# A mixture-of-experts decoder layer on one core: the experts' first matmul as three fp32r products, with their split weights streamed through a ring

## The chip, the cores and the metric

The kernel runs on one core of one Trainium2 chip. The metric is the device time of that core in microseconds, from one launch; lower is better. Engines are called by the names of the profile: PE is TensorE (PEld its weight loads), DVE is VectorE, ACT is ScalarE, POOL is GpSimd, SP is SyncE, whose queue issues most of the DMAs.

## The reference, cut to what matters

One decoder layer for 4 sequences of 512 tokens of width 256: causal attention, block-sparse cross attention of 16 heads, and a mixture of 8 experts with top-2 routing beside a shared expert. All in float32. The last part is the one that changes:

```python
xf = x.reshape(-1, DIM)                      # 2048 tokens x 256
logits = xf @ gate_w + gate_b
top_w, top_i = jax.lax.top_k(logits, K)      # 2 of 8 experts for each token
gw = jax.nn.softmax(top_w, axis=-1)
combine = (gw[:, :, None] * jax.nn.one_hot(top_i, E)).sum(axis=1)
for e in range(E):                           # w1[e]: 256 x 1024, w2[e]: 1024 x 256
    h = jax.nn.gelu(xf @ w1[e] + b1[e], approximate=False)
    out = out + combine[:, e:e + 1] * (h @ w2[e] + b2[e])
shared = jax.nn.gelu(xf @ ws1 + bs1, approximate=False) @ ws2 + bs2
return (out + shared).reshape(orig_shape)    # a layernorm follows
```

## The kernel before, in words

Every engine has a program of its own, written out by hand, and the engines meet at semaphores. There is no scheduler: an engine's instructions run in the order in which the code issues them.

**Attention.** Four "bodies" (`body(b, first, last)`), one for each sequence. Each does the cross attention of sequence b in two halves and between them the first attention of sequence b+1; at its end stands `project2`, which makes the queries, keys and values of the next body. In `project2` PE waits for `cb_out` before it spreads the queries (the matmul of L1570): `cb_out` is the end of `combine` on DVE (L1150 to L1161), which joins the outputs of the heads in `attn`. POOL splits the inputs of the next sequence into a high fp32r part and the rest (`split`, L422 and L425), adds a bias to the values (L508), helps in the layernorms (L479, L491, L494), and ends a body with `keep_x1` (L484) and `keep_x2` (L499).

**Three products.** In attention and in the shared expert a float32 product is made of three fp32r products: both operands are split into hi and lo, and `mm3` (L250) adds hi x hi, hi x lo and lo x hi in PSUM. The routed experts don't do so before: their matmuls (L1809, L1829) take float32 operands as they are.

**Shared expert.** The tokens go through it in 8 chunks of 256 (`shared_hidden`, `shared_output`). ACT does the gelu, DVE the splits (`x_split`, `h_split`, with `lo_of`, L861) and the sums (`y_out`). Its PE work covers the routing: DVE computes from the gate logits each token's slots (L1263 to L1313), then POOL scatters the 2048 rows twice to their slots in DRAM, 128 rows for each of 32 indirect DMAs (L582, the tile `slot_rows`), with at most four under way. SP then loads the first two tiles of rows (`xs`, L391), PE turns them (`turn_x`, L1792), and `shared_output` of the last chunk follows.

**Routed experts.** 4096 rows, sorted by expert and padded to tiles of 128, make TILES = 39 tiles; all 39 are computed. For a tile t PE does, in this order, `hidden(t+1)` (4 float32 matmuls of 512 columns, L1809; each is two records in the trace), `turn_x(t+2)` (2 transposes, L1792), `output(t)` (8 float32 matmuls of 256 columns, L1829) and `turn_h(t+1)` (8 transposes of `hp`, L1820). ACT copies the turned rows to `xT`, applies the gelu to the turned hidden rows (L815) and weights the result (L824); DVE copies the hidden rows out of PSUM (L1330) and adds the bias of the second layer (L1338); POOL adds the weighted rows to `row_sum` in DRAM (L597). The expert of a tile stands in `table`; PE loads it to a register (`expert(t)`) and addresses `we`, which holds all weights of all 8 experts (2 MB each), by it. SP loads experts 0 and 1 at the end of attention, experts 2 to 7 when the last chunk of the shared expert is done.

Of the kernel before, what the change touches and what calls it, by code (L numbers as in the profile page):

```python
# [54 lines left out]
EARLY = 2  # L55

# [16 lines left out]
def build(nc, x_d, xT_d, cT_d, w_d, brow_d, bcol_d, gate_w_d, gate_b_d,  # L73
          w1_d, b1T_d, w2_d, b2_d, ws1_d, bs1T_d, ws2_d, bs2_d, out_d):
    ctx = ExitStack()
    with ctx:  # L76
# [3 lines left out]
        def sem(name):  # L80
# [6 lines left out]
        q_rows = nc.dram_tensor("q_rows", (2, P, S), F, kind="Internal").ap()  # L87
        row_sum = nc.dram_tensor("row_sum", (T + P, D), F, kind="Internal").ap()
# [30 lines left out]
        shared = ExitStack()  # L119
        prod = sb("prod", [P, NT, D], F, shared)  # L120
        shared.close()
        v_s = sb("v_s", [P, 2, NT, D], FR, att)
        pT_s = sb("pT_s", [P, 2, NT * (NT + 1) // 2, P], FR, att)
# [6 lines left out]
        shift0 = sb("shift0", [P, 2], F, att)  # L130
        at_s = q_s
# [38 lines left out]
        we = sb("we", [P, E, EW], F, mo)  # L170
# [4 lines left out]
        xT = sb("xT", [P, 2, KD, P], F, mo)  # L175
# [22 lines left out]
        table = sb("table", [P, TILES], I32, mo)  # L198
        mo.close()
# [4 lines left out]
        sb("w2_home", [P, 24 * D], F, sh)  # L204
        ws1_s = sb("ws1_s", [P, 2, KD * HID], FR, sh)
        sb("at_home", [P, 2 * KD * S], F, sh)
        ws2_s = sb("ws2_s", [P, 2, NH * D], FR, sh)
        h_s = sb("h_s", [P, 2, NH, CT], FR, sh)
        h_full = sb("h_full", [P, NH, CT], F, sh)
# [12 lines left out]
        names = """x0_in x_in qk_in w1_in w2_in w1_hi w1_lo m_ps shift_step wvo_ps bvo bq_set bias_in b_in x_raw_in c_raw_in wsplit wsplit_hi consts consts2 masks q_zero xbo pad_set pad_out  # L222
          xa_split qk1_ps qk1_hi qk1_lo v1_ps v1_hi v1_lo s1_ps s1_raw s1_max s1_exp p1_den
          pt_ps pt_hi pt_lo w1_ps ln_res ln_step ln_pow x1_out x2_sub x2_out x_kept k_ones
          x1_ps x1_hi x1_lo ctx_split qk2_ps qk2_hi qk2_lo aug_in v_set
          a_ps a_red aug_step aug_ready augT_ps augT_out b_ps b_exp pv_done oc_out os_out
          sel_set parity_set sel_ps sel_act sel_dve
          cb_ps w_exp cb_step cb_out v2_ps v2_out at_ps at_hi at_lo w2_ps
          g_ps g_out lg_ps lg_out lgT_ps lgT_out
          ws_in we_in eb_in r_step r_exp r_exp_in r_ps table_ready slots_ready  # L230
          ws_split sxT_ps sx_split sh_ps sh_out sh_split sh_used sy_ps sy_sum sy_out kept_out
          xT_ps xT_out meta_in gate_set h_ps h_out hT_ps hT_out y_ps y_sum y_out y_idx
          f_step f_var f_pow f_bias f_out o_sent
# [4 lines left out]
        st_sent = [sem(f"s_st_sent{q}") for q in range(4)]  # L238
        k_away = [sem(f"s_k_away{h}_{part}") for h in range(2) for part in ("hi", "lo")]
# [16 lines left out]
        def _(sp):  # L256
# [21 lines left out]
            sp.wait_ge(s["pad_set"], 4)  # L278
# [42 lines left out]
            def body(b, first, last):  # L321
# [18 lines left out]
                if first:  # L340
                    sp.wait_ge(s["q_zero"], 1)
                else:
                    sp.wait_ge(s["b_ps"], 2 * UNITS * (2 * b))
# [21 lines left out]
            def load_expert(e):  # L365
# [6 lines left out]
            for e in range(EARLY):  # L372
                load_expert(e)
# [43 lines left out]
        def _(pool):  # L417
# [83 lines left out]
            def body(b, first, last):  # L501
# [20 lines left out]
                if not first:  # L522
                    keep_x2(b - 1)
# [1393 lines left out]
```

## Time and profile before

| | |
|---|---|
| median of 3 runs | 805.07 us (804.23 to 806.89) |
| the profiled execution | 804.36 us, span from first to last instruction 802.6 us |
| PE busy | 742.9 us, 93% of the span |
| DVE busy | 405.8 us, 51% |
| ACT busy | 331.6 us, 41% |
| POOL busy | 218.7 us, 27% |
| mean granted clock of TensorE | 0.969 |
| HBM read and written | 45.57 and 25.11 MB |

Read from it: PE is the engine that the whole program hangs on, from about 40 us to 780 us; the other engines matter where PE waits for them. Times in rows are microseconds from the first instruction.

### The profile page before, as it was taken

The page shows a single profiled execution, that of the slowest core. Times are in us where ns is not written, and L with a number is a line of the kernel's source. Part 1 is how long each engine was busy: PE and PEld are TensorE (multiplying, and loading weights), DVE is VectorE, ACT ScalarE, POOL GpSimd, SP SyncE. Part 2 cuts the span into 40 slices and gives each one's busy share as a digit, 9 for nine tenths or more (in the row PEclk, how much of TensorE's full clock was granted, in tenths as well). Part 3 has the DMA queues.
Part 4 walks back from the last instruction along what each step waited for, and adds up shares of the span by engine and source line. Part 5 has one row for each costly group of instructions (what it writes and reads, how often), then busy time and mean ns, then how long its engine had stood idle before and what let it go on. Part 6 is the DMA issues. An engine that isn't in the chain of part 4 may idle for free. (4 is left out here: it accounts for less than half of the span.)

```text
span 802.6 us, 14818 instructions
## 1 busy us (share of the span) xinstructions
PE 742.9 (93%) x4804; PEld 563.6 (70%) x4805; DVE 405.8 (51%) x807; ACT 331.6 (41%) x885; POOL 218.7 (27%) x217
## 2 busy tenths in 40 slices
PE   6689999999999999999999899999999999999960
PEld 5567666967696766669999856767676767676740
DVE  3767788787879766667875321212121212121214
ACT  1232556456636654463332124343434343434324
POOL 5762212151214103002078201212121212121223
PEclk9987999999999999999999999999999999999985
DMA  9952331405050713032133499412121212121216
GB/s 289 250 152 54 56 110 40 84 27 148 0 108 0 226 29 55 7 134 88 63 114 112 95 318 311 96 27 40 26 39 26 39 26 39 26 39 26 27 15 215
DMA packets 60489, 71.76 MB, mean 89 GB/s; under 512 B 15264, under 2 KB 49952, under 8 KB 59552
## 3 DMA queue, kind: packets, MB, share of 16 engines
q1 hardware_dynamic: 47968, 57.03, 25.8%
q0 software_dynamic: 7152, 9.34, 7.1%
q10 hardware_dynamic: 5328, 4.85, 2.2%
q8 instruction: 25, 0.41, 0.2%
q14 instruction: 16, 0.13, 0.1%
HBM read 45.57 MB, written 25.11 MB: 88 GB/s over the span
## 5 line engine op out<-in xcount | busy, mean ns | idle before, releaser
L815 ACT ACTIVATE hT<-ps,b1T 128x128 f32<-128x128 f32 x312 | 84.8, 383 | 167.2 <-PE ps L1820 167.1
L1829 PE MATMUL ps<-we,hT 128*128 x624 | 142.9, 383 | 2.5 <-ACT hT L815 2.5
L1809 PE MATMUL ps<-we,xT 128*128 x312 | 140.5, 593 | 0.3 <-issue 0.3
L1829 PEld LDWEIGHTS ps<-we,hT 128*128 128x128 f32 x624 | 117.0, 192 | 17.6 <-issue 3.2
L1330 DVE COPY hp<-ps 128x512 f32<-128x512 f32 x78 | 50.3, 686 | 146.5 <-PE ps L1809 146.5
L1103 DVE TENSOR_REDUCE mx<-ps 128x4 f32<-128x512 f32 (+1 forms) x128 | 103.6, 819 | 20.6 <-PE ps L1627 19.4
L1809 PEld LDWEIGHTS ps<-we,xT 128*128 128x128 f32 x312 | 56.3, 191 | 56.4 <-issue 56.4
L726 ACT ACTIVATE pT<-ps 128x256 f32<-128x256 f32 x128 | 49.1, 384 | 69.7 <-PE ps L1643 59.5
L1627 PE MATMUL ps<-k_stack,q_stack 96*128 96x256 f32 (+1 forms) x256 | 72.3, 368 | 5.2 <-DVE mx L1103 3.0
L592 POOL CAST yidx<-meta 128x1 int32<-128x1 f32 x39 | 7.2, 184 | 234.8 <-ACT yw L824 234.8
L597 POOL DMA_INDIRECT row_sum<-yw,yidx x39 | 60.9, 1560 | 30.5 <-issue 26.4
L1338 DVE TENSOR_TENSOR ysum<-ps,b2b 128x256 f32<-128x256 f32 x39 | 16.6, 425 | 103.3 <-PE ps L1829 103.3
L1627 PEld LDWEIGHTS ps<-k_stack,q_stack 96*128 96x128 f32 x256 | 40.1, 197 | 33.4 <-issue 19.1
L729 ACT ACTIVATE pT<-ps 128x256 f32<-128x256 f32 (+1 forms) x128 | 62.4, 487 | 0.1
L250 PE MATMUL ps<-ws_s,h_s 128*128 128x256 f32 x384 | 48.6, 288 | 0.0
L250 PE MATMUL ps<-xT_s,ws_s 128*128 128x256 f32 x384 | 48.2, 285 | 0.0
L250 PEld LDWEIGHTS ps<-ws_s,h_s 128*128 128x128 f32 x384 | 47.7, 196 | 0.0
L250 PEld LDWEIGHTS ps<-xT_s,ws_s 128*128 128x128 f32 x384 | 46.6, 192 | 0.2 <-issue 0.2
L1649 PE MATMUL ps<-q_stack,k_stack 98*128 98x256 f32 (+1 forms) x128 | 46.3, 362 | 0.0
L582 POOL DMA_INDIRECT slot_rows<-XW,slot_tab x32 | 36.8, 1150 | 30.1 <-DVE slot_tab L1313 20.9
L775 ACT ACTIVATE h_full<-ps,b1T 128x256 f32<-128x256 f32 x64 | 26.4, 473 | 39.5 <-PE ps L250 39.5
L1820 PE MATMUL ps<-ident,hp 128*128 128x128 f32 x312 | 40.5, 273 | 1.4 <-DVE hp L1330 1.4
(238 smaller groups left out, 1083.7 us busy)
## 6 DMA issues: line engine op xcount, KB each, us to landing
we<-in_w SPq DMA_DIRECT2D x16, 1024.0 KB, 8.9
k_stack<-k_rows SPq DMA_DIRECT2D x24, 256.0 KB, 4.8
slot_rows<-attn SPq DMA_DIRECT2D x1, 4992.0 KB, 24.5
xs<-slot_rows ACTq DMA_DIRECT2D x37, 128.0 KB, 2.0
k_rows<-k_s SPq DMA_DIRECT2D x16, 256.0 KB, 2.1
q_stack<-q_rows SPq DMA_DIRECT2D x48, 64.0 KB, 5.6
x_raw<-in_xT SPq DMA_DIRECT2D x4, 512.0 KB, 5.1
XW<-in_x SPq DMA_DIRECT2D x4, 512.0 KB, 8.5
```

The source lines that it names most:

```text
L250: m = nc.tensor.matmul(out, lhs(a), rhs(b), start=first and n == 0, stop=last and n == 2, skip_group_check=check)
L597: pool.indirect_dma_start(out=row_sum, out_offset=bass.IndirectOffsetOnAxis(ap=yidx[:, q, :], axis=0), in_=yw[:, q, :], in_offset=None, co ...
L726: nc.scalar.activation(pT[:, m % 2, u % 2, 0:2 * P], ps[:, bank, 256:512], ACT.Exp, scale=SCALE2)\
L729: nc.scalar.activation(pT[:, m % 2, u % 2, 2 * P:2 * P + w], ps[:, bank + 1, 0:w], ACT.Exp, scale=SCALE2).then_inc(s["b_exp"], 1)
L815: last = nc.scalar.activation(hT[:, c, :], ps[:, 4 + c // 4, (c % 4) * P:(c % 4 + 1) * P], ACT.Gelu, bias=b1T[:, bass.ds(e * NH + c, 1)])
L1103: nc.vector.tensor_reduce(mx[:, i, 2 * p:2 * p + 2, r0:r0 + nb], ps[:, 2 * ((u + flip) % 2):2 * ((u + flip) % 2) + 2, 0:nb * P].rearrange( ...
L1330: last = nc.vector.tensor_copy(hp[:, c * 512:(c + 1) * 512], ps[:, 2 + c, :])
L1627: m = nc.tensor.matmul(ps[:, 2 * ((u + flip) % 2) + j, 0:nb * P], q_stack[0:96, ha * HALF + PAIRS * j + p, n * P:(n + 1) * P], k_stack[0:9 ...
L1649: nc.tensor.matmul(ps[:, bank + 1, 0:w].rearrange("p (h n q) -> p h n q", h=2, q=P), k_stack[0:98, p, i * P:(i + 1) * P], qv[0:98, :, :].r ...
L1809: m = nc.tensor.matmul(ps[:, 2 + c, :], xT[:, q, k, :], w[:, bass.ds(e, 1), k * HID + c * 512:k * HID + (c + 1) * 512].rearrange("p o n -> ...
L1820: m = nc.tensor.transpose(ps[:, 4 + c // 4, (c % 4) * P:(c % 4 + 1) * P], hp[:, c * P:(c + 1) * P], ident[:, :])
L1829: m = nc.tensor.matmul(ps[:, 6, 0:D], hT[:, c, :], w[:, bass.ds(e, 1), KD * HID + c * D:KD * HID + (c + 1) * D].rearrange("p o n -> p (o n)"),
```

## The change

The first layer of the routed experts (`hidden`) becomes three fp32r products with `mm3`, like the shared expert's. For that the weights w1 of each expert must lie split, hi and lo, and they take twice the room. So:

- `we` is replaced by `w1r`, a ring of four places for split w1 (2 MB each), and `w2r`, which holds w2 of all experts. A new table `places` says where an expert's weights lie; PE loads from it once for `hidden` and once for `output`.
- Split w1 of experts 2 to 7 are made on the way and kept in DRAM (`w1_split`): experts 2 to 4 by POOL, one at the end of each of the first three bodies (`w1_load`, `w1_parts`, `w1_save`); experts 5 to 7 in chunks 4 to 6 of the shared expert, hi by ACT and lo by DVE. Experts 0 and 1 are split in the ring itself: hi by ACT, lo by POOL (`first_lo`, once ahead of a `norm_pow`, once ahead of the scatter).
- SP stores and loads the parts; a place of the ring is filled again when all tiles of the expert in it are through `hidden` (`tile_end`).
- The turned rows `xT` get a lo part too, by DVE (`x_lo`).
- Some semaphores are merged, some SBUF is laid out anew, POOL's loop over bodies is written out, and `prod` in attention holds two rows and not four.

The core of the diff, with all that is spoken of below:

```diff
@@ block.sync @@
+            def load_w1(e):
+                sp.dma_start(w1r[:, e % RING, :, :].bitcast(F), w1_split[e]).then_inc(s["we_in"], 16)
+            def save_w1(e, nth, hi, lo, done):
+                sp.wait_ge(s["w_hi"], nth + EARLY)
+                sp.dma_start(w1_split[e, :, 0, :], hi[:, :].bitcast(F)).then_inc(done, 16)
+                sp.wait_ge(s["w_lo"], nth)
+                sp.dma_start(w1_split[e, :, 1, :], lo[:, :].bitcast(F)).then_inc(done, 16)
...
-            for c in range(CHUNKS - 3):
+            for c in range(CHUNKS - 4):
                 rows_kept(c)
+            save_w1(5, 1, hi_c, lo_c, w_saved[1])
+            sp.wait_ge(w_saved[1], 32)
+            raw_w1(7, raw_c[:, :], w_raw[1])
+            rows_kept(CHUNKS - 4)
+            save_w1(6, 2, hi_d, lo_d, w_saved[2])
+            sp.wait_ge(w_saved[2], 32)
+            for e in range(EARLY):
+                load_w2(e)
             for q in range(4):
                 sp.wait_ge(st_sent[q], 16 * 2 * T // P // 4)
...
+                if e >= RING:
+                    sp.wait_ge(s["h_ps"], sp.value_load(tile_end[0:1, e - RING:e - RING + 1], min_val=1, max_val=TILES + 1))
+                load_w1(e)
+                load_w2(e)
@@ block.gpsimd @@
+            def w1_load(n):
+                pool.wait_ge(s["w1_ps"], 2 * n + 4)
+                if n:
+                    pool.wait_ge(w_saved[0], 32 * n)
+                pool.dma_start(raw_a[:, :].rearrange("p (k n) -> p k n", k=KD),
+                               w1_d[EARLY + n].rearrange("(k p) n -> p k n", p=P)).then_inc(w_raw[0], 16)
+            def w1_parts(n):
+                pool.wait_ge(w_raw[0], 16 * n + 16)
+                nc.gpsimd.tensor_copy(hi_a, raw_a[:, :]).then_inc(s["w_split"], 1)
+                pool.wait_ge(s["w_split"], 2 * n + 1)
+                nc.gpsimd.tensor_tensor(lo_a, raw_a[:, :], hi_a.bitcast(F), ALU.subtract).then_inc(s["w_split"], 1)
+            def w1_save(n):
+                pool.wait_ge(s["w_split"], 2 * n + 2)
+                for l, part in enumerate((hi_a, lo_a)):
+                    pool.dma_start(w1_split[EARLY + n, :, l, :], part.bitcast(F)).then_inc(w_saved[0], 16)
+            def first_lo(e):
+                pool.wait_ge(s["w_hi"], e + 1)
+                nc.gpsimd.tensor_tensor(w1r[:, e, 1, :], raw_ring[:, e, 1, :], w1r[:, e, 0, :].bitcast(F), ALU.subtract)\
+                    .then_inc(s["w_split"], 1)
             def body(b, first, last):
                 if not last:
                     split(a_s, x_raw, ...)
+                if not first:
+                    w1_save(b - 1)
...
                 if not last:
+                    w1_load(b)
                     split(c_s, c_raw, ...)
...
                 if not first:
                     keep_x2(b - 1)
+                if not last:
+                    w1_parts(b)
@@ block.scalar @@
             copy(at_s[:, 0, :, :], ps[:, 2:4, :], "at_hi")
+            for e in range(EARLY):
+                act.wait_ge(s["raw_in"], 16 * EARLY)
+                copy(w1r[:, e, 0, :], raw_ring[:, e, 1, :], "w_hi")
...
+                if c in (4, 5, 6):
+                    act.wait_ge(w_raw[(1, 2, 1)[c - 4]], (16, 16, 32)[c - 4])
+                    copy((hi_c, hi_d, hi_c)[c - 4][:, :], (raw_c, raw_d, raw_c)[c - 4][:, :], "w_hi")
@@ block.vector @@
-            link(nc.vector.tensor_scalar(table[:, :], tab_f[:, :], float(E - 1), None, ALU.min))
+            link(nc.vector.tensor_scalar(tab_f[:, :], tab_f[:, :], float(E - 1), None, ALU.min))
+            nc.vector.tensor_copy(table[:, :], tab_f[:, :])
...
+                if c in (4, 5, 6):
+                    dve.wait_ge(s["w_hi"], EARLY + c - 3)
+                    lo_of((lo_c, lo_d, lo_c)[c - 4][:, :], (raw_c, raw_d, raw_c)[c - 4][:, :], (hi_c, hi_d, hi_c)[c - 4][:, :],
+                          "w_lo")
...
+                def x_lo(t, q):
+                    dve.wait_ge(s["xT_out"], t + 1)
+                    lo_of(xT[:, q, 1, :, :], ps[:, 7 * q, 0:KD * P].rearrange("p (k t) -> p k t", k=KD),
+                          xT[:, q, 0, :, :], "xT_lo")
@@ block.tensor @@
-                def hidden(t, q, e):
-                    pe.wait_ge(s["xT_out"], t + 1)
+                def hidden(t, q):
+                    e, at = expert(t), place(0, t)
+                    weights(e)
+                    pe.wait_ge(s["xT_lo"], t + 1)
                     if not (isinstance(t, int) and t == 0):
                         pe.wait_ge(s["h_out"], t)
                     for c in range(2):
                         for k in range(KD):
-                            m = nc.tensor.matmul(
-                                ps[:, 2 + c, :], xT[:, q, k, :],
-                                w[:, bass.ds(e, 1), k * HID + c * 512:k * HID + (c + 1) * 512].rearrange("p o n -> p (o n)"),
-                                start=k == 0, stop=k == KD - 1)
+                            cols = slice(k * HID + c * 512, k * HID + (c + 1) * 512)
+                            m = mm3(pe, ps[:, 2 + c, :], lambda l: xT[:, q, l, k, :],
+                                    lambda l: w1r[:, bass.ds(at, 1), l, cols].rearrange("p o n -> p (o n)"),
+                                    k == 0, k == KD - 1)
```

On PE, inside the loop over tiles, this is what stood between the last matmul of `output(t)` and the first of `hidden(t+2)` before (ISA rows are register arithmetic for addresses, L1801 and L1804 belong to the wait for weights):

```order
L1829 MATMUL ps<-we,hT 128x256
L1801 ISA
L1820 MATMUL ps<-ident,hp 128x128 x8
L1804 REGISTER_ALU
L1809 ISA
L1809 MATMUL ps<-we,xT 128x512
```

And now, from behind the same eight transposes (L1944) on:

```order
L1916 ISA
L1916 TENSOR_LOAD table
L1916 ISA x2
L1923 REGISTER_ALU
L1923 TENSOR_LOAD places
L1923 ISA x2
L1920 ISA
L1928 REGISTER_ALU
L273 ISA
L273 MATMUL ps<-w1r,xT 128x512
L273 ISA
L273 MATMUL ps<-w1r,xT 128x512 x2
```

Two loads of a register from SBUF have come between `turn_h` and `hidden` (L273 is `mm3`); a third one stands ahead of `output`. Before, there were three such loads in two tiles, now there are six.

On POOL, at the end of a body in the loop, before:

```order
L483 REGISTER_ALU [waits s_aug_ready]
L484 ISA [waits s_x1_out]
L484 TENSOR_TENSOR XW<-res,brow 128x4x256
L499 ISA [waits s_x2_out]
L499 COPY XW<-res 128x4x256
L534 REGISTER_ALU
L534 COMPARE_AND_BRANCH
```

And now, with the start of the next body behind it:

```order
L536 TENSOR_TENSOR XW<-res,brow 128x4x256 [waits s_x1_out,s_aug_ready]
L551 COPY XW<-res 128x4x256 [waits s_x2_out]
L562 CAST pT_s<-raw_a 128x2048 [waits s_w_rawa]
L564 TENSOR_TENSOR v_s<-raw_a,pT_s 128x2048 [waits s_w_split]
L474 TENSOR_TENSOR a_s<-x_raw,zero 128x1024 [waits s_qk2_ps,s_x_raw_in]
L477 TENSOR_TENSOR a_s<-x_raw,a_s 128x1024 [waits s_xa_split]
L569 DMA w_split<-pT_s 128x2048 [waits s_w_split]
L569 DMA w_split<-v_s 128x2048
```

A copy and a subtraction of 2048 elements in each partition now follow right behind `keep_x2`; their parts lie in the tiles `pT_s` and `v_s`.

On POOL ahead of the scatter, before (constants for the routing, then the first indirect DMA):

```order
L555 CAST desc<-r_t 128x8
L556 CAST step<-r_lg 128x16
L558 CAST tile_no<-table 128x39
L559 CAST XW<-r_mask 128x16
L582 DMA slot_rows<-XW,slot_tab 4992x258 [waits s_slots_ready,s_pad_out,s_consts2]
```

And now:

```order
L637 CAST desc<-r_t 128x8
L638 CAST step<-r_lg 128x16
L640 CAST tile_no<-table 128x39
L641 CAST XW<-r_mask 128x16
L574 TENSOR_TENSOR w1r<-raw_ring,w1r 128x2048 [waits s_w_hi]
L665 DMA slot_rows<-XW,slot_tab 4992x258 [waits s_routed,s_pad_out,s_consts]
```

The subtraction of `first_lo(1)` has come between the constants and the scatter.

## Rows read from the trace of the kernel before

**Rows 1.** Busy time by stage: us, each engine's busy us (count), clock, DMA, GB/s

```profile
450.30:466.80 16.50, 12.52 (x68) 9.81 (x69) 6.38 (x9) 0.77 (x2) 0.00 (x0) 0.90 0.71 165
466.80:779.50 312.70, 308.74 (x1308) 215.44 (x1306) 65.56 (x115) 114.49 (x388) 66.49 (x77) 0.99 0.30 67
```

**Rows 2.** Timeline of one expert tile: start, us, instruction, count [idle before]

```profile
522.71 3.60 PE L1809 MATMUL ps<-we,xT 128*128 x8
...
523.03 2.17 ACT L815 ACTIVATE hT<-ps,b1T 128x128 f32<-128x128 f32 x8 [4.06 <-PE ps L1820]
...
526.14 0.38 PE L1792 MATMUL ps<-ident,xs 128*128 128x128 f32 x2
...
526.36 3.62 PE L1829 MATMUL ps<-we,hT 128*128 x16
...
530.69 3.60 PE L1809 MATMUL ps<-we,xT 128*128 x8
```

**Rows 3.** Timeline of PE: fp32r matmuls of 512 columns in attention, and what follows

```profile
142.19 3.02 PE L250 MATMUL ps<-a_s,w_s 128*128 128x512 f32 x12
145.04 0.60 PE L1412 MATMUL ps<-ident,aug 128*32 128x128 f32 x4
...
185.00 1.62 PE L250 MATMUL ps<-c_s,w_s 128*128 128x512 f32 x6
186.46 0.60 PE L1412 MATMUL ps<-ident,aug 128*32 128x128 f32 x4
```

**Rows 4.** Timeline of POOL and of DVE, about 203 us

```profile
202.56 2.44 POOL L425 TENSOR_TENSOR a_s<-x_raw,a_s 128x1024 fp32r<-128x1024 f32 x1
...
203.29 1.99 DVE L1084 TENSOR_TENSOR prod<-XW,u_row 128x256 f32<-128x256 f32 x1
...
205.81 0.41 DVE L1084 TENSOR_TENSOR prod<-XW,u_row 128x256 f32<-128x256 f32 x1
```

**Rows 5.** A group of POOL: busy us, mean ns of one | idle us before

```profile
L425 POOL TENSOR_TENSOR c_s<-c_raw,c_s 128x1024 fp32r<-128x1024 f32 x4 | 9.5, 2374 | 0.3
```

**Rows 6.** Timeline at the ends of bodies 1 and 0; a wait: us, times

```profile
186.92 1.04 POOL L499 COPY XW<-res 128x1024 f32 x1
...
191.35 0.19 DVE L1154 TENSOR_TENSOR cw<-wloc,cw 128x32 f32<-128x32 f32 x1
...
107.33 2.38 POOL L484 TENSOR_TENSOR XW<-res,brow 128x1024 f32<-128x1024 f32 x1 [5.66 <-DVE aug L1125]
...
114.28 0.19 DVE L1154 TENSOR_TENSOR cw<-wloc,cw 128x32 f32<-128x32 f32 x1
...
PEld ps L1570 <- DVE attn L1161: 2.3, 3, 1.4
```

**Rows 7.** Timeline of the routing and of the end of the scatter

```profile
380.95 0.21 POOL L559 CAST XW<-r_mask 128x16 f32<-128x16 int32 x1
...
383.55 0.29 DVE L1201 TENSOR_TENSOR r_t<-logits,r_m 128x128 f32<-128x128 f32 x1
...
447.50 0.96 POOL L582 DMA_INDIRECT slot_rows<-XW,slot_tab  x1 [0.30 <-issue]
...
452.56 1.23 PE L1792 MATMUL ps<-ident,xs 128*128 128x128 f32 x4 [2.30 <-DMA xs<-slot_rows]
```

**Rows 8.** Timeline: subtractions by DVE, and an indirect DMA issued beside one

```profile
404.47 1.23 DVE L861 TENSOR_TENSOR h_s<-h_full,h_s 128x1024 fp32r<-128x1024 f32 x1
404.99 1.55 POOL L582 DMA_INDIRECT slot_rows<-XW,slot_tab  x1 [0.30 <-issue]
...
348.01 2.29 DVE L861 TENSOR_TENSOR ws_s<-ws,ws_s 128x2048 fp32r<-128x2048 f32 x1
```

**Rows 9.** DMA issues: count, KB, median us to landing; 470 to 485 us, then all

```profile
row_sum<-yw,yidx POOLq DMA_INDIRECT x1, 9.5
...
slot_rows<-XW,slot_tab POOLq DMA_INDIRECT x32, 2.8
row_sum<-yw,yidx POOLq DMA_INDIRECT x39, 3.8
```

More of the change, by code:

```diff
@@ L55 @@
 EARLY = 2
+RING = 4
+W2_AT = 2
+ATT_EXPERTS = B - 1
 WARM = 24
@@ L198, in build @@
         table = sb("table", [P, TILES], I32, mo)
+        tab_s = sb("tab_s", [P, 2, TILES], F, mo)
+        places = sb("places", [P, 2, TILES], I32, mo)
+        tile_end = sb("tile_end", [P, E], I32, mo)
+        xT = sb("xT", [P, 2, 2, KD, P], FR, mo)
         mo.close()
@@ L533, in _ @@
             body(0, True, False)
-            with pool.Fori(1, B - 1) as b:
+            for b in range(1, B - 1):
                 body(b, False, False)
             body(B - 1, False, True)
+            first_lo(0)
             norm_pow(2 * B - 1, 1)
@@ L563, in _ @@
-            pool.wait_ge(s["consts2"], 12)
+                .then_inc(s["consts"], 1)
+            first_lo(1)
+            pool.wait_ge(s["consts"], 27)
             pool.wait_ge(s["pad_out"], 48)
-            pool.wait_ge(s["slots_ready"], 1)
+            pool.wait_ge(s["routed"], 1)
             HALF_ROWS = T // P // 2
@@ L662, in glue_and_attention1 @@
                 if n is not None:
+                    if g is not None:
+                        act.wait_ge(w_saved[0], 32 * (g + 1))
                     for j in range(2):
@@ L1311, in _ @@
             nc.vector.tensor_copy(XW[:, :, D + 1], r1["g1"][:, :])
-            for k, sl in enumerate(("s1", "s2")):
-                last = nc.vector.tensor_copy(slot_tab[:, :, k], r1[sl][:, :])
-            last.then_inc(s["slots_ready"], 1)
-            nc.vector.tensor_copy(r1["m2"][:, :], r1["g1"][:, :]).then_inc(s["table_ready"], 1)
+            for n, sl in enumerate(("s1", "s2")):
+                last = nc.vector.tensor_copy(slot_tab[:, :, n], r1[sl][:, :])
+            last.then_inc(s["routed"], 1)
+            for i, wrap in enumerate((RING, E - W2_AT)):
+                link(nc.vector.tensor_scalar(tab_s[:, i, :], tab_f[:, :], float(wrap), -float((RING, E)[i]), ALU.is_ge, ALU.mult))
+                nc.vector.scalar_tensor_tensor(out=places[:, i, :], in0=tab_f[:, :], scalar=float((0, W2_AT)[i]),
+                                               in1=tab_s[:, i, :], op0=ALU.add, op1=ALU.add)
+            nc.vector.tensor_scalar(tile_end[:, :], end_e[:, :], 1.0, None, ALU.add).then_inc(s["routed"], 1)
             x_split(4)
@@ L1345, in expert_tiles @@
                     h_out(t + 1)
+                    x_lo(t + 2, t)
                     y_sum(t, t, False)
@@ L1349, in expert_tiles @@
                         h_out(2 * i + q + 1)
+                        x_lo(2 * i + q + 2, q)
                         y_sum(2 * i + q, q, True)
@@ L1353, in expert_tiles @@
                         h_out(t + 1)
+                    if t + 2 < TILES:
+                        x_lo(t + 2, t % 2)
                     y_sum(t, t % 2, True)
@@ L1822, in turn_h, with output @@
                     m.then_inc(s["hT_ps"], 1)
-                def output(t, e):
+                def output(t):
+                    at = place(1, t)
                     pe.wait_ge(s["hT_out"], t + 1)
```

244 lines of the change are left out of this document (132 added, 112 removed).

## The prediction

> **What bounds the kernel now.** I read the busy time by stage first. In the experts' stage PE is busy 308.7 of 312.7 us at a clock of 0.99, all other engines under 40% [rows 1]: 39% of the span hangs on PE alone. The timeline of one tile says of what it is made: `hidden` 522.71 to 526.14, 3.43 us; the two transposes 0.22; `output` and `turn_h` up to the next `hidden` at 530.69, 4.33; together 7.98 us, without a gap [rows 2]. The gelu that `output` waits for runs from 523.03 to 525.20, beside `hidden`, and is done 1.2 us before `output` starts at 526.36 [rows 2].
>
> Before that stage the bound changes hands. PE waits 2.30 us for `xs` [rows 7], so there the path is: routing on DVE, 32 scatters on POOL, the load of `xs`. Whatever delays that chain delays the end; PE's own work has 2.3 us to spare. In attention PE is nearly always busy, and at the ends of bodies it waits for `combine` on DVE (L1161 to L1570, 2.3 us in three waits) [rows 6]: DVE's lateness at that place is PE's.
>
> **The change, part by part.**
>
> *The gain.* `hidden` goes from 4 float32 matmuls to 12 fp32r ones of 512 columns. Twelve such in attention take 145.04 - 142.19 = 2.85 us, six take 186.46 - 185.00 = 1.46 [rows 3]; the second six add 1.39, so each costs 0.232 us and the start some 0.07, which in the loop can hide behind the transposes. `hidden` becomes 12 x 0.232 = 2.78 us (bounds 2.70 and 2.85). Saved: 0.65 a tile, in 39 tiles 25.4 us (22.6 to 28.5).
>
> The records of a float32 matmul fit a rule of the Trainium skill ("FP8 and Floating Point Precision", section "TensorE Precision Notes"): a float32 product takes 4 passes through the array, reduced precision works on a shortened operand. One pass each would make three products 3/4 of 3.43, 2.57 us, and the gain 33.5 us; the sum below would be 8 us lower. The rows of this case, which have the real matmuls of that shape, say 2.78, and I go by them.
>
> What must keep up with the shorter tile of 7.33 us: the gelu must be done 2.78 + 0.22 = 3.0 us after `hidden` starts, it is at 2.5 [rows 2]; DVE has 66 of 313 us busy [rows 1], `x_lo` adds an operation of about 0.4 a tile. Both stay hidden, with 0.5 us to spare in the first. The three loads of registers a tile lie on PE's sequencer, which runs ahead; I cost them at nothing, see the rivals. The ring is no bound on average: 39 tiles for 8 experts are 36 us an expert, a place is filled again two experts or more ahead of need.
>
> *The cost in attention.* `w1_parts` puts a copy and a subtraction of 2048 elements on POOL right behind `keep_x2`. POOL has room; DVE has not. A DVE operation with two operands in SBUF, `prod`, takes 0.41 us alone, but started at 203.29 beside POOL's subtraction it took 1.99 and ended at 205.28, 0.28 behind POOL's end at 205.00 [rows 4]. It stood still until POOL's instruction was through. The skill ("SBUF — State Buffer", section "SBUF: two separate sides") states just this: such a DVE operation and a GpSimd one take a port pair by an exclusive lock, for the whole instruction.
>
> POOL's subtraction of 1024 takes 2.37 [rows 5], so of 2048 about 4.75; the copy of 1024 takes 1.04 [rows 6], so of 2048 about 2.1. In body 1 POOL is free at 187.96, the copy ends at 190.0, the subtraction at 194.8. `combine` reaches its first operation with two SBUF operands at 191.35 [rows 6] and stands until 194.8: 3.4 us. PE waits for `combine` there, so PE loses it too. Body 2 has the same pattern: 3.4. In body 0 POOL is free at 109.71, the subtraction ends at 116.5, `combine` is at that place at 114.28 [rows 6]: 2.3. Together 9.1 us. Bounds: nothing, if DVE slips in first or if the lag is made up, and 14.2, if each hits a whole subtraction. The rows 4 show the full wait, so I take 9.1. The loads and saves of POOL (`w1_load`, `w1_save`) come where it idles; behind `w1_load` are queued the split of `c_s` and the layernorm's steps, with some us of slack.
>
> *The cost in routing.* `first_lo(0)` comes some 4 us before POOL is next wanted; nothing. `first_lo(1)` starts when the constants are done, 380.95 + 0.21 = 381.16, and lasts to 385.9; DVE's routing starts its first operation with two SBUF operands at 383.55 [rows 7]: 2.4 us late, and the chain has no slack. One operation more ahead of `slot_tab`: 0.2. Together 2.6 (0 to 5). ACT's two copies of 2048 delay its gelu of chunk 1 by some 4 us, whose results are wanted 7 us later: nothing. The steps for `places` delay PE's chunk 4, within PE's spare time.
>
> *The cost in the scatter.* DVE's three subtractions for experts 5 to 7 run while POOL issues the scatter. An indirect DMA takes POOL 0.96 us [rows 7] and 1.55 beside a DVE subtraction of 1.23 [rows 8]: 0.6 more. The new ones take 2.29 [rows 8]: 1.1 more each in proportion, 1.65 if POOL waits for the rest of the lock; three cost 3.3 to 5, I take 4.5 (0 to 6.9). And 9 transfers of 1 MB (one raw, six parts, two w2) now run in the 46 us of the scatter. A scatter lands after 2.8 us in a quiet time; an indirect DMA among the loads of weights landed after 9.5 [rows 9]. Four may be under way, issued 1.26 apart, which covers a landing of about 4 to 5 us. I take 2.5 us in all (0 to 20).
>
> *The clock.* With these 9.6 us on the chain, and PE's work 2.5 later at most, PE idles some 7 us more at 450 us. It idled 2.3 there and the stretch shows a clock of 0.90 [rows 1]; a longer idle time leaves more of the last chunk's matmuls at the lower of the two levels. I add 1.0 (0 to 3).
>
> *Sum*, against the span of 802.6: - 25.4 + 9.1 + 2.6 + 4.5 + 2.5 + 1.0 = 796.9 us. The profiled execution is 1.8 us above its span, 798.7, and the median of the runs 0.7 above that execution: **799 us**.
>
> **Rivals.**
>
> - *The main case*, these terms in about these sizes: 792 to 804. Chance 0.50.
> - *The locks cost little.* DVE's and POOL's operations meet otherwise than the old times say, since the first delay shifts all behind it, or the lag at body ends is made up by DVE's slack later in the body. Then the 9.1 and the 4.5 go nearly to nothing: 787. For it: PE has some 2% of idle time in bodies. Against it: rows 4, and the wait of rows 6. Chance 0.14.
> - *One pass a product*, as by the page on precision: a matmul at 512 columns costs 0.214 and not 0.232, the rest of rows 3 being an effect of attention. `hidden` 2.57, gain 33.5: 791. But then the gelu ends only 0.3 us before `output` is ready for it. Chance 0.10.
> - *Slower: bulk transfers hold the scatter.* Each of the 9 transfers of 1 MB stops the scatter by 1.5 us or more, as the landing of 9.5 hints: 13.5 and not 2.5, that is 810. It decides against the change from 0.95 us each on (8.5 in all, 805). Against it: loads are issued one at a time, each waiting for the part before, where rows 9 had 12 at once. Chance 0.13.
> - *The change doesn't do what it says: PE waits for its sequencer.* Two register loads and the address arithmetic now stand between `turn_h` and `hidden`. If 0.34 us a tile shows, half the gain is gone: 812. For it: six loads in two tiles where there were three. Against it: the loop has 4.3 us of queued work in `output` and `turn_h` while they run. Chance 0.08.
> - Others, 0.05 on either side.
>
> **How the numbers follow.** The time is that of the main case, 799. The range is 788 to 806: it leaves out the upper part of the two slow rivals and a thin lower end. No change is within 0.3%, 802.65 to 807.5, about what a measurement of this kernel can tell. Faster: nearly all of the main case (0.43), the second and third (0.24), some of the others: 0.70. Same: the tail of the main case and the mild form of the slow rivals: 0.13. Slower: 0.17.
>
> **What the profile after would show.** Right: `hidden` takes 2.7 to 2.85 us in the timeline and a tile 7.3; the last operations of `combine` start when POOL's 2048 subtraction ends, at three body ends, and PE's wait for `attn` grows from some 0.8 us to about 4 at two of them; the routing's first operation takes over 2 us; the scatter lasts some 52 us and not 46; PE waits some 9 us for `xs`. Wrong would be: a gap before each `hidden` (sequencer), a gap before each `output` (gelu), scatters that wait for landings (DMA), or `combine` at its old pace beside a busy POOL.

## The result, and the profile after

The changed kernel takes 807.54 us (median of 18 runs) where the kernel before takes 805.64 us beside it (18 runs). The ratio of the runs is 1.0036, interval 1.0019 to 1.0054: slower by 0.4%, where 799, faster by 0.8%, was predicted. The profiled execution took 809.14 us, its span 807.1.

The gain came in full. The timeline of PE in the experts, in the changed kernel (start, duration, engine, line, operation):

```profile
546.32 3.03 PE L273 MATMUL ps<-w1r,xT 128*128 x12
549.18 0.38 PE L1911 MATMUL ps<-ident,xs 128*128 128x128 f32 x2
549.40 3.62 PE L1954 MATMUL ps<-w2r,hT 128*128 x16
552.85 1.04 PE L1944 MATMUL ps<-ident,hp 128*128 128x128 f32 x8
553.64 3.03 PE L273 MATMUL ps<-w1r,xT 128*128 x12
```

`hidden` is 12 records from 546.32 to the transposes at 549.18, 2.86 us, and PE is never idle. A tile is 553.64 - 546.32 = 7.32 us where it was 7.98 [rows 2]. Tile by tile the two traces come 0.65 us closer. Yet the windows of the changed kernel show what [rows 1] did not: idle time and a lower granted clock ahead of the experts' stage (after the stretch: busy us of PE, PEld, DVE, ACT, POOL with instruction counts, granted clock, DMA share, GB/s):

```profile
70.00:353.00 283.00, 265.56 (x2235) 197.81 (x2233) 217.79 (x430) 149.29 (x351) 81.59 (x46) 0.98 0.37 100
402.00:450.00 48.00, 45.49 (x369) 45.31 (x368) 38.53 (x73) 19.46 (x37) 24.98 (x22) 0.96 0.39 138
450.00:480.00 30.00, 18.91 (x149) 18.48 (x148) 13.53 (x16) 6.14 (x12) 13.60 (x13) 0.82 0.71 222
```

The kernel before is busy for 272.68 us of the first of these stretches, at a clock of 1.00. The waits of the changed kernel name two places (engine, what it waits for, us in total, times, longest), and both are new in size:

```profile
PE ps L1689 <- DVE attn L1256: 8.3, 3, 2.8
PE ps L1911 <- DMA xs<-slot_rows: 11.1, 1, 11.1
```

**The sum as it came.** I compare the start of the same matmul in both traces, which splits the difference of the spans, 4.5 us; the last line takes what is left over:

| term | predicted | measured | how read |
|---|---|---|---|
| `hidden` shorter, 39 tiles | -25.4 | -25.5 | 0.654 a tile |
| `combine` locked, 3 body ends | +9.1 | +7.3 | PE's waits there, longer by 1.81 + 2.73 + 2.77 |
| PE slow behind that wait, and the rest of attention | 0 | +4.7 | first transpose of the shared expert 336.95, now 349.00: 12.0 in all |
| routing | +2.6 | +2.1 | scatter starts at 416.20, was 402.10: 14.1 in all |
| scatter: POOL's own time | +4.5 | +1.0 | 37.8 us for 36.8 |
| scatter: waits | +2.5 | +10.1 | it lasts 57.5 us, was 46.4 |
| behind the wait for `xs` | +1.0 | +3.9 | 27.6 late at the third `turn_x`, with two gains of 0.65 added back 28.9; 25.0 at the first |
| tail and rounding | 0 | +0.9 | |
| sum | -5.7 | +4.5 | |

**The lock** is as foretold. At the end of body 1 POOL's subtraction ran from 192.96 for 4.59 us, and the operation of `combine` that takes 0.19 us in [rows 6] took 2.95, to 197.59, 0.04 behind POOL's end. DVE, then POOL, in the changed kernel:

```profile
194.64 2.95 DVE L1249 TENSOR_TENSOR cw<-wloc,cw 128x32 f32<-128x32 f32 x1
197.62 0.69 DVE L1250 TENSOR_TENSOR cmb<-ps,cw 128x512 f32<-128x512 f32 x1
...
192.96 4.59 POOL L564 TENSOR_TENSOR v_s<-raw_a,pT_s 128x2048 fp32r<-128x2048 f32 x1
```

**What I did not foresee is behind it.** PE waits 2.77 us, and then its eight matmuls take 3.56 us. In the kernel before they take 2.09. The windows show why: the granted clock is at 0.50 for 3 us, the lower of the two levels (1.2 GHz and not 2.4).

```profile
199.92 3.56 PE L1689 MATMUL ps<-q_s,w_s 128*96 128x512 f32 x8 [2.77 <-DVE attn L1256]
```

```profile
199.00:200.00 1.00, 0.08 (x1) 0.08 (x1) 0.97 (x4) 0.00 (x0) 0.00 (x0) 0.87 0.01 2
200.00:203.00 3.00, 3.00 (x7) 1.98 (x8) 2.30 (x4) 1.42 (x3) 0.00 (x0) 0.50 0.51 188
203.00:205.00 2.00, 2.00 (x17) 1.93 (x16) 1.79 (x3) 1.09 (x2) 0.00 (x0) 0.96 0.93 241
```

**The routing** is late as foretold. Its first operation with two operands in SBUF took 2.31 us and not 0.29, beside `first_lo(1)` on POOL:

```profile
395.59 2.31 DVE L1296 TENSOR_TENSOR r_t<-logits,r_m 128x128 f32<-128x128 f32 x1
```

**The scatter** stands still three times, each time until an earlier scatter has landed (its rows are in DRAM and its semaphore has counted). Bulk transfers are under way meanwhile: the saves of expert 5 from 436.7 to 445.5, the raw load and the saves of expert 6 from 445.5 to 459.4, the loads of w2 from 459.4 on. Beside them a scatter lands up to 9.9 us after its issue; the ones before take 2.5 to 4.5. POOL in the changed kernel:

```profile
446.41 0.96 POOL L665 DMA_INDIRECT slot_rows<-XW,slot_tab  x1 [3.17 <-DMA slot_rows<-XW,slot_tab]
...
460.01 1.83 POOL L665 DMA_INDIRECT slot_rows<-XW,slot_tab  x1 [4.81 <-DMA slot_rows<-XW,slot_tab]
...
468.66 1.17 POOL L665 DMA_INDIRECT slot_rows<-XW,slot_tab  x1 [2.66 <-DMA slot_rows<-XW,slot_tab]
```

PE waits 11.1 us for `xs`, and again pays with the lower level. The last `shared_output` takes 8.0 us; it took 7.0 in the kernel before, which waited 2.3, and the other chunks take 5.9. The second `hidden` (493.54) takes 4.5 us and not 3.0. PE in the changed kernel:

```profile
478.46 8.01 PE L273 MATMUL ps<-ws_s,h_s 128*128 128x256 f32 x48
487.37 3.06 PE L273 MATMUL ps<-w1r,xT 128*128 x12 [0.91 <-issue]
...
493.54 4.49 PE L273 MATMUL ps<-w1r,xT 128*128 x12 [0.63 <-issue]
```

Of the 3.9 us by which this stretch got longer the clock has 2.4. Another 1.2 is idle time ahead of the first two `hidden`, for which the profile names no releaser: 0.91 and 0.63 us, where the kernel before had 0.34 and nothing. The new register loads stand at this place, but no run tests whether they are the cause.

### The profile page after: what moved, and what is told of

It reads as the page before. It is cut to its first block and busy times, and to the rows that moved or that the text cites. A ratio compares the mean times of both kernels' runs of the same rounds, so it can differ in the third digit from the quotient of the medians.

```text
span 807.1 us, 15577 instructions
## 1 busy us (share of the span) xinstructions
PE 726.5 (90%) x4960; PEld 598.7 (74%) x4961; DVE 435.1 (54%) x854; ACT 340.8 (42%) x890; POOL 254.6 (32%) x234
## 3 DMA queue, kind: packets, MB, share of 16 engines
q0 software_dynamic: 8832, 18.78, 10.1%
## 5 line engine op out<-in xcount | busy, mean ns | idle before, releaser
L1954 PE MATMUL ps<-w2r,hT 128*128 x624 | 142.9, 383 | 2.5 <-ACT hT L906 2.5
L1954 PEld LDWEIGHTS ps<-w2r,hT 128*128 128x128 f32 x624 | 116.7, 192 | 17.4 <-issue 2.7
L273 PE MATMUL ps<-w1r,xT 128*128 x468 | 119.5, 404 | 1.5 <-issue 1.5
L273 PEld LDWEIGHTS ps<-w1r,xT 128*128 128x128 f32 x468 | 86.3, 191 | 19.4 <-issue 2.0
L680 POOL DMA_INDIRECT row_sum<-yw,yidx x39 | 61.0, 1564 | 34.9 <-issue 25.4
L273 PE MATMUL ps<-xT_s,ws_s 128*128 128x256 f32 x384 | 49.7, 290 | 0.0
L665 POOL DMA_INDIRECT slot_rows<-XW,slot_tab x32 | 37.8, 1181 | 37.3 <-DVE tile_end L1419 18.5
L273 PE MATMUL ps<-ws_s,h_s 128*128 128x256 f32 x384 | 49.5, 291 | 0.0
L273 PEld LDWEIGHTS ps<-ws_s,h_s 128*128 128x128 f32 x384 | 48.7, 200 | 0.0
L273 PEld LDWEIGHTS ps<-xT_s,ws_s 128*128 128x128 f32 x384 | 48.1, 197 | 0.2 <-issue 0.2
L1944 PE MATMUL ps<-ident,hp 128*128 128x128 f32 x312 | 40.5, 273 | 1.4 <-DVE hp L1438 1.4
L1944 PEld LDWEIGHTS ps<-ident,hp 128*128 128x128 f32 x312 | 36.4, 141 | 5.7 <-DVE hp L1438 1.8
## 6 DMA issues: line engine op xcount, KB each, us to landing
slot_rows<-attn SPq DMA_DIRECT2D x1, 4992.0 KB, 25.5
```

The lines of the kernel that those rows point to most:

```text
L273: m = nc.tensor.matmul(out, lhs(a), rhs(b), start=first and n == 0, stop=last and n == 2, skip_group_check=check)
L665: pool.indirect_dma_start(out=slot_rows, out_offset=bass.IndirectOffsetOnAxis(ap=slot_tab[:, t, k:k + 1], axis=0), in_=XW[:, t, :], in_off ...
L680: pool.indirect_dma_start(out=row_sum, out_offset=bass.IndirectOffsetOnAxis(ap=yidx[:, q, :], axis=0), in_=yw[:, q, :], in_offset=None, co ...
L1944: m = nc.tensor.transpose(ps[:, 4 + c // 4, (c % 4) * P:(c % 4 + 1) * P], hp[:, c * P:(c + 1) * P], ident[:, :])
L1954: m = nc.tensor.matmul(ps[:, 6, 0:D], hT[:, c, :], w2r[:, bass.ds(at, 1), c * D:(c + 1) * D].rearrange("p o n -> p (o n)"), start=c == 0, ...
```

## The experiments

The runs form four groups, each on one chip with the kernel before timed beside it. In the first two groups the kernel before took 830.9 and 829.3 us, in the last two 804.7 and 805.6. In the traces of the first two, PE has gaps in the shared expert, idle times with no releaser, which are told of at the end. Times are compared within a group, and where the gaps cover a difference, the traces decide.

**Base.** The changed kernel was run in the second and the fourth group.

> The changed kernel itself once more, beside the three of this call, since the chip of the last call stopped PE for 8 to 28 us inside the sixth chunk of the shared expert in every kernel, with no wait that the profile shows. Where that stall is absent: 806 to 809 and a ratio of 1.002 to 1.005; where it is there, both kernels carry it and this run tells how much.

> The changed kernel beside the others of this call, as the base of their ratios. On a chip without PE's gaps in the shared expert: 806 to 809, ratio to the kernel before 1.002 to 1.005. On one with them: 806 to 810, ratio about 0.976.

Measured: 808.0 (ratio to before 0.976) and 808.3 us (1.0038, 1.0013 to 1.0063). In the second group the kernel before is slower than elsewhere and the changed kernel is not, so ratios to the kernel before say nothing about the change there.

**The lock: the subtraction behind `combine`.**

```diff
                 pool.wait_ge(s["w_split"], 2 * n + 1)
+                pool.wait_ge(s["cb_out"], 2 * n + 1)
                 nc.gpsimd.tensor_tensor(lo_a, raw_a[:, :], hi_a.bitcast(F), ALU.subtract)...
```

> The changed kernel, but POOL's subtraction in w1_parts waits until combine on DVE is through (cb_out). Theory (the lock stops combine for 1.8, 2.8 and 2.8 us, and PE, idle meanwhile, then runs its next matmuls at the lower clock level): the second operation of combine with two SBUF operands takes 0.2 us again, the eight matmuls behind the wait 2.1 and not 3.4 us, attention ends some 12 us earlier, median about 795.5, ratio to the kernel before about 0.988. Rival 1 (the slow matmuls have another cause, such as the loads of raw weights): only the 7.3 us of the lock come back, about 800, ratio 0.993. Rival 2 (the subtraction stops whatever DVE does next): about 807, ratio 1.002.

Measured: 821.4 us (four runs from 805.0 to 826.1) beside a kernel before of 830.9, in a group with gaps of PE, so the total says nothing. The trace does: the operation of `combine` takes 0.19 us, the subtraction runs from 119.56 on, when `combine` is through, and the matmuls behind the wait are fast again (seven of the eight stand in this window).

```profile
116.95 0.19 DVE L1250 TENSOR_TENSOR cw<-wloc,cw 128x32 f32<-128x32 f32 x1
119.56 4.62 POOL L565 TENSOR_TENSOR v_s<-raw_a,pT_s 128x2048 fp32r<-128x2048 f32 x1 [5.35 <-DVE attn L1257]
119.47 1.88 PE L1690 MATMUL ps<-q_s,w_s 128*96 128x512 f32 x7 [0.96 <-DVE attn L1257]
```

At the three body ends PE's wait and the eight matmuls behind it are 3.1, 4.2 and 3.8 us shorter, 11.1 in sum: the theory is right about the lock and what it costs, and both rivals are wrong. But attention did not end 12 us earlier. Some 8 us are given back, for the clock stays at 0.50 from 135 to 155 us. That was new, and is taken up below.

**Is it the clock? Fill PE's wait.** `keep_clock(10)` is ten matmuls of 512 columns whose results nobody reads.

```diff
+                    pe.wait_ge(s["qk2_lo"], 4 * b + 1)
+                    keep_clock(10, bank=6)
                     pe.wait_ge(s["cb_out"], c + 1)
```

> The changed kernel, with ten matmuls of no use on PE ahead of its wait for combine at body ends; the lock and the 7.3 us that combine is late are left as they are. Theory (PE idle for 2.7 to 3 us falls to the lower clock level and then runs the next matmuls slowly): the eight matmuls behind the wait take 2.1 us and not 3.4, attention ends 4 to 5 us earlier, 803 in all, ratio to the changed kernel 0.995. Rival (the clock falls for another reason, such as the transfers): no difference, ratio 1.000.

Measured: 805.9 us beside 808.0 for the changed kernel on the same chip. The lock is as before, the ten matmuls stand in the wait, and the eight behind it take 2.09 us:

```profile
115.48 2.43 PE L1507 MATMUL ps<-w_s 128*128 128x512 f32 x10
118.39 2.09 PE L1691 MATMUL ps<-q_s,w_s 128*96 128x512 f32 x8 [0.49 <-DVE attn L1256]
```

Over the three body ends the matmuls behind the wait give back 3.4 us, and attention ends 3.6 us earlier than in the changed kernel's trace of this group (344.91 for 348.46). So most of the 4.7 us is the clock after an idle time of 2.8 us, not a transfer. The whole kernel gained 2.1 us and not the expected 5 (ratio to the changed kernel 0.997), with PE's gaps in both.

**The scatter: eight under way.** The semaphores of the four and of four others that were done by then; the copies of the second gates stand two places later.

```diff
-                if n >= 4:
-                    pool.wait_ge(st_sent[n % 4], 16 * (n // 4))
+                if n >= 8:
+                    pool.wait_ge(st_sent[n % 8], st_base[n % 8] + 16 * (n // 8))
```

> The changed kernel with up to eight scatters under way and not four. Theory (the scatter's 10 us of waits are late landings behind bulk transfers, a latency that more scatters under way cover): the scatter lasts 47 to 49 us and not 57.5, PE waits 1 to 3 us for xs, and with less idle time less of the lower clock: 796 to 799, ratio 0.989 to 0.992. Rival (the engines of the DMA are full, so that the rows can't be moved sooner whatever is queued): the waits stay, 806 to 808.

> The changed kernel with eight scatters under way, once more: in the last call PE's stall made the saves come behind the scatter, so that it did not meet them. Theory (late landings are a latency): no wait over 1 us between scatters although the saves lie among them, the scatter 47 to 49 us, 796 to 799 in all. Rival (bandwidth): waits of 5 us or more in sum and 804 to 808.

Measured: 822.6 and 815.5 us (ratios 0.987 and 0.986), both in groups with gaps. The second is 7.5 us slower than the changed kernel beside it (808.0), where 796 to 799 was expected: the gaps are longer in its trace (23 us lost against 13). No scatter waited over 0.4 us, but in both PE's gaps held DVE back, so that none or one pair of the saves met the scatter. These two don't decide between latency and bandwidth. The versions below, with the same edit and the same transfers beside the scatter as in the changed kernel, do.

**Saves cut to 64 columns, w2 loaded behind `xs`** (experts 5 and 6 use the parts of expert 4).

> The changed kernel with the four saves of experts 5 and 6 cut to 64 columns (experts 5 and 6 then use the parts of expert 4) and the two loads of w2 moved behind the load of xs; one load of 1 MB stays in the scatter. Theory (bulk transfers hold the scatters' landings): no scatter waits over 1 us, save perhaps one at the load that stays, and the scatter lasts 47 to 50 us. Rival (DVE's lock starves POOL, or POOL's own queue is slow): the three waits of 3.2, 4.8 and 2.7 us stay and it lasts 55 us or more.

**DVE's three subtractions replaced by memsets** (the lo parts of experts 5 to 7 are zero).

> The changed kernel with DVE's three subtractions of 2048 elements for experts 5 to 7 replaced by memsets (lo parts are zero). Theory (three scatters are stretched by the lock, 1.9, 0.9 and 0.9 us): no scatter takes over 1.6 us, the scatter lasts 53 to 56 us, the waits for landings stay. Rival (the lock is what starts the waits): it lasts under 50 us.

Measured: 803.9 and 821.0 us, one run each, in the first group, where the changed kernel was not run. The row of the scatter in three kernels (instructions, busy us, mean ns, idle before them by releaser; the first idle share is routing): the changed kernel, then without the saves, then with memsets.

```profile
L665 POOL DMA_INDIRECT slot_rows<-XW,slot_tab x32 | 37.8, 1181 | 37.3 <-DVE tile_end L1419 18.5 <-DMA slot_rows<-XW,slot_tab 10.8 <-issue 8.1
```

```profile
L666 POOL DMA_INDIRECT slot_rows<-XW,slot_tab x32 | 38.1, 1192 | 27.6 <-DVE tile_end L1420 18.4 <-issue 7.8 <-DMA slot_rows<-XW,slot_tab 1.2
```

```profile
L665 POOL DMA_INDIRECT slot_rows<-XW,slot_tab x32 | 33.3, 1041 | 27.6 <-DVE tile_end L1419 18.4 <-issue 7.5 <-DMA slot_rows<-XW,slot_tab 1.5
```

Without the saves the waits for landings go from 10.8 to 1.2 us at the same busy time: the scatter lasts 48.4 us, as the theory has it. Part of this may be the gaps: in the second group, with gaps, the changed kernel itself waits only 4.9 us (two waits, a scatter of 49.7), and its saves come later. And the saves and the loads of w2 went in one edit, so this run doesn't tell them apart. The run with memsets is inconclusive: PE's gaps, 28 us in it, put DVE's steps behind the scatter, so nothing met it at all.

**Three edits together**: the later subtraction, eight scatters, and

```diff
             first_lo(0)
+            first_lo(1)
             norm_pow(2 * B - 1, 1)
```

> Three edits together: the subtraction of w1_parts behind combine, first_lo(1) right behind first_lo(0), eight scatters under way. Theory (each cost is separate: 12 us in attention, 2 in the routing, 10 in the scatter, 3 of the low clock behind the wait for xs): attention ends as in the kernel before, the scatter lasts 47 to 49 us, PE waits 2 to 5 us for xs, and the median is 780 to 784, ratio to the kernel before 0.968 to 0.974. Rival (the transfers share a bandwidth that the scatter needs, or the subtraction hits another place): 789 to 795, ratio 0.980 to 0.987.

> The version with three edits once more, since PE's gaps in the shared expert covered what it gained. On a chip without the gaps: 780 to 790, ratio to the kernel before 0.970 to 0.980. On one with them: 802 to 814 as before.

Measured: 812.1 us (0.975) in the group with gaps, 4 us slower than the changed kernel beside it, and 797.4 us (0.991, 0.988 to 0.994) in one without. In the latter the saves and the loads lie beside the scatter, scatters land up to 9.2 us after their issue, and yet it lasts 46.8 us:

```profile
L667 POOL DMA_INDIRECT slot_rows<-XW,slot_tab x32 | 37.0, 1156 | 31.9 <-DVE tile_end L1421 22.6 <-issue 7.6 <-DMA slot_rows<-XW,slot_tab 1.2
```

So late landings are a latency that more of them under way cover. But 797 is not 781. About half of the difference is the low clock in the attention of sequence 0 again. Another part is the routing, where the third edit gained nothing. Its first operation is fast again, 0.29 us, but DVE now waits for a load just behind it, and the scatter starts 67.2 us after the shared expert's first transpose, as in the changed kernel (65.2 before). The same wait, 1.7 to 2.4 us, is in every trace with this edit. DVE in the run of 797.4:

```profile
394.89 0.29 DVE L1298 TENSOR_TENSOR r_t<-logits,r_m 128x128 f32<-128x128 f32 x1
...
401.54 0.69 DVE L1325 TENSOR_TENSOR ws<-ps,b2b 128x512 f32<-128x512 f32 x1 [1.69 <-DMA b2b<-in_b]
```

**w2 behind `xs`.**

> The version with three edits, and the two loads of w2 of experts 0 and 1 moved from the scatter to behind the loads of xs (output of tile 0 comes 16 us later). Theory (with eight scatters under way no transfer holds the scatter any more): same time as the version with three edits, within 2 us. Rival (w2 then comes too late): PE waits ahead of the first output, 3 to 8 us slower.

Measured: 797.2 us (0.987, 0.981 to 0.993), the same. PE waited 2.0 us for `xs` and not 5.2, but then 3.8 for w2, since `hidden` of tile 0 waits for it: both theories in part, and they cancel.

**The low stretch: the order of `shift_piece`.** With `prod` of two rows the change had put a product and a sum into each of three slots between the `mx` that PE waits for; before, one step stood in each of eight slots.

```diff
-                if 2 <= u < 2 + NT:
-                    t = u - 2
+                if u in (2, 3, 5, 7):
+                    t = (2, 3, 5, 7).index(u)
...
-                if 3 <= u < 3 + NT:
-                    t = u - 3
+                if u in (4, 6, 8, 9):
+                    t = (4, 6, 8, 9).index(u)
```

> The version with three edits, and DVE's steps of shift_piece so ordered that one stands in each of eight slots, as in the kernel before, though prod keeps its two rows (products in slots 2, 3, 5, 7, sums in 4, 6, 8, 9; the changed kernel has two steps in each of slots 3 to 5). Theory (those second steps hold mx back, PE waits 1.2 us at once, and the granted clock then stays at the lower level from 132 to 152 us, which costs 8 us): no stretch at the lower level there, 788 to 791, ratio to the kernel before 0.978 to 0.984. Rival (the low stretch has another cause, the later subtraction on POOL or the loads): it stays, 795 to 799.

> The changed kernel with only the later subtraction of w1_parts and the order of shift_piece. Theory (both costs in attention gone, the scatter as in the changed kernel): 12 us faster than the changed kernel, 795 to 797, ratio to it 0.985 to 0.987. Rival (the low stretch stays): 4 us faster, 803 to 804.

Measured: 788.7 us (0.979, 0.976 to 0.982) with the three edits and the order, and 795.0 us (0.988, 0.984 to 0.992) with the later subtraction and the order alone, 19.6 and 13.3 us under the changed kernel beside them. The window of the stretch in the version with three edits, and with the order added:

```profile
132.00:152.00 20.00, 18.63 (x135) 11.18 (x133) 12.60 (x24) 8.44 (x21) 1.40 (x3) 0.60 0.26 106
```

```profile
132.00:152.00 20.00, 19.96 (x179) 15.30 (x176) 15.84 (x36) 9.56 (x24) 0.00 (x0) 1.00 0.35 102
```

In 20 us PE does 135 matmuls at a granted clock of 0.60, and 179 at 1.00. All four traces with the later subtraction and the old order have the low stretch, the three with the new order don't. In the changed kernel the same steps cost only some 0.5 us.

**The wait for `xs`, filled.** The order, w2 behind `xs`, `hidden` of tile 0 not waiting for it, and:

```diff
+                pe.wait_ge(s["routed"], 2)
+                keep_clock(16, ws2_s[:, 0, 0:512], 2)
                 turn_x(0, 0)
```

> The version with three edits and the order of shift_piece, and besides: the loads of w2 of experts 0 and 1 behind the load of xs, hidden of tile 0 not waiting for them, and 16 matmuls of no use ahead of PE's wait for xs. Theory (idle time ahead of xs leaves PE at the lower level for the last chunk and the first tile, 3 to 4 us): shared_output of the last chunk takes 5.9 us and not 7, hidden of tile 0 under 3 us, and 3 to 6 us less than the version without them: 783 to 787. Rival (the gap is filled but the clock falls anyway, or w2 is waited for further on): within 1 us of it.

Measured: 785.3 us, ratio to the kernel before 0.975 (0.971 to 0.978), 23 us under the changed kernel of the same group, 3.4 under the version without the last edits. The kernel before did not get those of the edits that would fit it too, such as a filled wait for `xs`, so 785.3 beside 805.6 is not the worth of the changed `hidden` alone. PE in it:

```profile
454.30 3.82 PE L1509 MATMUL ps<-ws_s 128*128 128x512 f32 x16
457.96 0.60 PE L1913 MATMUL ps<-ident,xs 128*128 128x128 f32 x4
458.31 5.99 PE L275 MATMUL ps<-ws_s,h_s 128*128 128x256 f32 x48
464.14 2.94 PE L275 MATMUL ps<-w1r,xT 128*128 x12
```

The last `shared_output` takes 5.99 us, not 8.0. The second `hidden` still takes 4.4 us, behind a wait of 1.4 us for `hp` and another 1.4 us idle with no releaser. This version beats both kernels.

**PE's gaps.**

> The kernel before itself, for its profile on the chip of this call. Theory (on the two chips so far the kernel before took 829 to 831 us and not 805, because PE is fed slowly inside the scatter as in the traces of the changed kernel there, and it has only 2.3 us to spare): PE shows gaps with no wait in the sixth chunk of the shared expert, 20 us or more in sum, and no wait for xs. Rival (another stage is slower on these chips): no such gaps, and the time is lost elsewhere. On a chip like the first: 805.

> The changed kernel with the scatter held until the shared expert's last gelu, so that PE's chunks 4 to 7 run without a scatter beside them; the end comes later by the scatter's length, some 40 us. Theory (PE's gaps with no wait come from the scatter that POOL issues): each half of a chunk takes 5.9 to 6.0 us, without gaps. Rival (they belong to a block of instructions, or to the chip, whatever runs beside): gaps of 8 us or more in the sixth chunk as before.

Measured: 806.3 and 837.6 us (the latter one run), in a group without the gaps. Neither could show what it was made for. The kernel with the scatter held has halves of chunks of 6.0 and 5.9 us without gaps, but so has every kernel there.

## Why the prediction was wrong

- **The gain** was right to 0.1 us, and it was worked out from rows of attention. `hidden` itself is 2.86 us and not 2.78, but the stretch from the start of `output` to the next `hidden` went from 4.33 to 4.24, which makes up for the start of 0.07 that I let hide. One pass a product, which would have saved 0.86 a tile, is refuted. No tile waited for the sequencer or for the gelu in the loop, so what I costed at nothing cost nothing there. Ahead of the first two tiles PE idled 1.2 us more than before.
- **The lock in attention** was right in place and mechanism, 7.3 for 9.1. The size was off because POOL's copy took 1.90 us and not 2.1, its subtraction 4.6 and not 4.75, and DVE came to the place 0.2 us later after POOL in two of the bodies. The rule of the Trainium skill that I cited ("SBUF — State Buffer", "SBUF: two separate sides") is borne out: DVE's operation ended 0.04 us behind POOL's.
- **The step that failed first** is "PE waits for `combine` there, so PE loses it too": PE loses more. I charged an idle time with its length; each of 2.8 us cost another 1.0 to 1.5 at the lower level, 3.8 us in the 24 matmuls behind `combine`. I had this term only for the wait at `xs`, and gave it 1.0; there it was 2.4. So the lower clock cost 6.2 us where I had 1.0 in all.
- **The step that failed most in one term** is "I take 2.5 us in all" for the transfers beside the scatter. It was 10.1. The rival "bulk transfers hold the scatter" had the mechanism, from the landing of 9.5 in [rows 9], and priced it at 13.5. I held against it that loads are issued one at a time. They are not: two saves overlap (issued at 436.7 and 438.5), and so do the two loads of w2 (459.4 and 459.9), and a pair was enough to make a landing later than the 5 us that four under way cover. I also miscounted: seven transfers of 1 MB lie beside the scatter and not nine, since the parts of expert 7 are saved behind it (479.5 on). They cost 1.4 us each, where I had put the deciding point at 0.95 for each of nine.
- **Some of it was luck.** My 4.5 for the locks on POOL's issue was 1.0: the three instructions that met them took 3.7 us more, but fewer of the others met DVE. With the 1.8 us of the lock in attention that is 5.3 us charged too much. Without this the sum would have missed by 15 us and not by 10.
- **Routing** was right, 2.1 for 2.6, and by its mechanism: 2.0 of it is the lengthened first operation. That does not mean that taking the lock away gives it back, as the three edits showed.
- **One edit was not costed at all**: `prod` with two rows. It costs 0.5 us here, and 7 to 9 us once the other delay in front of it is gone.

## What to carry to other kernels

When a wait of TensorE grows by microseconds and TensorE is the bound engine, charge it twice: its length, and the stretch at the lower clock behind it; a trace of before that never idles shows neither. When bulk transfers are put beside small ones with a fixed number under way, ask how late one may land before the issuer stops, and raise that number first. When an edit takes a delay away, look at what the engine waits for next: here a load took the place of the lock. When buffers shrink, look at where the steps that reuse them now stand between the ones that the bound engine waits for.

## What was not expected of the hardware

In the first two groups of runs PE falls behind within the sixth chunk of the shared expert, from about 430 us on: short bursts of matmuls with idle times of 0.1 to 3.1 us, for which the profile shows no releaser. The changed kernel in the second group:

```profile
432.88 1.00 PE L273 MATMUL ps<-xT_s,ws_s 128*128 128x256 f32 x5 [0.37 <-issue]
434.32 0.62 PE L273 MATMUL ps<-xT_s,ws_s 128*128 128x256 f32 x3 [0.45 <-issue]
435.74 0.52 PE L273 MATMUL ps<-xT_s,ws_s 128*128 128x256 f32 x3 [0.81 <-issue]
...
443.57 0.37 PE L273 MATMUL ps<-xT_s,ws_s 128*128 128x256 f32 x1 [1.31 <-issue]
```

The first half of that chunk took 13.8 to 34.4 us in the eight traces taken there, and 6.0 in all others: 8 to 28 us lost. Only part of that, 4 to 20 us, is idle time; meanwhile the granted clock fell to 0.50 too, in the trace above from 438.6 to 452.3. The changed kernel hid it in its wait of 11 us for `xs`, of which 0.6 was left, and kept its 808 us. The kernel before, which has 2.3 us to spare, took 25 us more, but no trace of it was taken there, so that the gaps are its cause is argued and not shown. What feeds PE slowly stays open: whether the scatter does was tried once, in a group that has no gaps. Nor is it shown that the gaps belong to a chip, for the record gives the chips of the first group, with gaps, and of the fourth, without, the same number, 15.

Nor had I expected that idle times of 0.9 to 1.3 us in attention, with sparse work behind them, would be followed by 17 to 20 us at the lower level, where 2.8 us ahead of dense work were followed by 3. Their length does not decide: at the same place the version with the new order waits 0.98 us and the changed kernel 0.71, 0.31 and 0.21, and the clock stays at 1.00 in both. Under the later subtraction the order of DVE's steps brings the stretch or keeps it away, but what on PE decides is not settled.
